# Small 32-bit products of layer 1: moving operand repeated to 96 columns

## The reference, cut to what matters

```python
# Mamba-2: 8 heads
dt = zxbcdt[..., D_INNER + CONV_DIM:]          # 8 columns of x @ in_proj_w.T
dt = softplus(dt + dt_bias); dA = exp(dt * A)  # decays: the kernel uses running sums of dt * A
y = y * rsqrt(mean(y * y, axis=-1) + 1e-05) * norm_w
# mLSTM: 4 heads
gate_in = concatenate([q, k, v], axis=-1)      # k and v are both ctx
ig = gate_in @ igate_kernel + igate_bias       # 4 columns
fg = gate_in @ fgate_kernel + fgate_bias       # 4 columns
cs = cumsum(log_sigmoid(fg), axis=tokens)
```

## Time and profile before

| | |
|---|---|
| median of 3 runs | 1158.27 us (1157.61 to 1158.8) |
| the profiled execution, own time | 1157.71 us |
| its span | 1156.0 us |
| PE busy | 1109.2 us, 96% |
| DVE busy | 824.5 us, 71% |
| ACT busy | 671.1 us, 58% |
| chain that ended last | PE 80%, DVE 11%, ACT 6% |
| mean granted TensorE clock | 0.986 of full |

### The profile page before, as it was taken

One profiled execution on the slowest core, in us unless ns is written; L12 is line 12 of the kernel. 1 busy time (PEld: TensorE's weight loads), 2 busy tenths in 40 slices (PEclk: granted clock), 3 DMA queues, 4 the chain that ended last, 5 costly groups with the idle time before them and its releaser, 6 DMA issues.

```text
span 1156.0 us, 23649 instructions
## 1 busy us (share of the span) xinstructions
PE 1109.2 (96%) x8692; PEld 922.6 (80%) x8692; DVE 824.5 (71%) x2589; ACT 671.1 (58%) x1423; POOL 324.6 (28%) x354
## 2 busy tenths in 40 slices
PE   7999999999999999999999999989999999999996
PEld 6778888768888877888867888868788887888875
DVE  5825558884668783668883767898797877887673
ACT  4237555236665436656425765586558866678573
POOL 5699956990037100026300003302000001000000
PEclk9999999999999999999999999998999989999999
DMA  8200000100000100000100201210000101000000
GB/s 335 113 19 1 2 1 1 56 20 1 2 1 2 55 20 1 2 2 2 37 20 5 73 1 46 69 51 1 2 19 2 47 1 29 19 2 28 28 20 19
DMA packets 21393, 33.33 MB, mean 29 GB/s; under 512 B 11424, under 2 KB 12192, under 8 KB 20128
## 3 DMA queue, kind: packets, MB, share of 16 engines
q1 hardware_dynamic: 21280, 31.82, 8.1%
HBM read 27.62 MB, written 4.19 MB: 28 GB/s over the span
## 4 chain that ended last, share of the span: by engine, by line
PE 80%; DVE 11%; ACT 6%; issue 2%; POOL 0%; DMA 0%; DVEq 0%; SPq 0%; ACTq 0%
PE ps L498 48%; PE ps L654 4%; PE ps L672 2%; PE ps L671 2%; PE ps L646 2%; DVE z L1631 2%; PE ps L644 2%; PE ps L670 2%; PE ps L914 2%; PE ps L513 1%; PE ps L610 1%; PE ps L701 1%; PE ps L874 1%; DVE pq L1475 1%; PE ps L623 1%
## 5 line engine op out<-in xcount | busy, mean ns | idle before, releaser
L498 PE MATMUL ps<-wts,arena 128*128 128x256 f32 (+2 forms) x1008 | 196.0, 350 | 4.8 <-ACT arena L1392 2.7
L2150 POOL TENSOR_TENSOR pq<-pq 128x512 f16<-128x512 f32 x72 | 83.9, 1166 | 406.0 <-ACT pq L1239 406.0
L498 PE MATMUL ps<-arena,wts 128*128 128x256 f16 (+1 forms) x1344 | 184.6, 290 | 8.6 <-DVE arena L1445 6.3
L498 PEld LDWEIGHTS ps<-wts,arena 128*128 128x128 f32 (+1 forms) x1008 | 149.8, 151 | 40.1 <-ACT arena L1392 3.2
L498 PEld LDWEIGHTS ps<-arena,wts 128*128 128x128 f16 (+1 forms) x1344 | 149.6, 113 | 30.4 <-DVE arena L1445 6.7
L1631 DVE SCALAR_TENSOR_TENSOR z<-ps,small,z 128x256 f32<-128x256 f32 x256 | 123.9, 484 | 22.9 <-PE ps L498 6.0
L1516 DVE CUSTOM_DVE_ANT_0 pq<-ps,mb 128x128 f32<-128x128 f32 x128 | 36.9, 288 | 106.2 <-PE ps L646 105.6
L498 PE MATMUL ps<-wts,pq 128*128 128x256 f16 x864 | 106.4, 273 | 4.5 <-DVE z L1631 1.7
L2198 POOL TENSOR_TENSOR z<-z,wts 128x512 f32<-128x512 f32 x8 | 10.3, 1282 | 318.3 <-PE ps L513 318.3
L498 PEld LDWEIGHTS ps<-wts,pq 128*128 128x128 f16 x864 | 83.4, 98 | 17.8 <-POOL pq L2150 3.4
L1236 ACT ACTIVATE pq<-ps 128x512 f32<-128x512 f32 x72 | 42.8, 595 | 83.8 <-PE ps L498 83.3
(11 more groups left out here) (290 smaller groups left out, 2488.9 us busy)
## 6 DMA issues: line engine op xcount, KB each, us to landing
cT<-in_cT SPq DMA_DIRECT2D x16, 256.0 KB, 2.7
wts<-in_up SPq DMA_DIRECT2D x1, 2304.0 KB, 18.4
wts<-in_down SPq DMA_DIRECT2D x1, 2304.0 KB, 23.8
xT<-in_xT SPq DMA_DIRECT2D x8, 256.0 KB, 4.1
xin<-in_x SPq DMA_DIRECT2D x8, 256.0 KB, 2.9
xmid<-xin SPq DMA_DIRECT2D x8, 256.0 KB, 2.0
wts<-in_w SPq DMA_DIRECT2D x2, 1024.0 KB, 4.9
wts<-in_c SPq DMA_DIRECT2D x16, 128.0 KB, 3.1
```

The costliest lines, as they stand in the source:

```text
L498: ins = mm(out_, l, r, start=(n == 0), stop=(n == len(pairs) - 1))
L2150: G.tensor_tensor(lo, abuf(s, e), hi, ALU.subtract).then_inc(*po.up(("alo", s, e)))
```

## The change

In layer 1 every product of the five steps above streams 96 columns where it streamed 8, 4 or 1. For `dt`, `gates` and the running sums the moving operand is the same 8 or 4 columns named 12 or 24 times by an access pattern with a step of 0 (`repeated`); nothing more is stored in SBUF. For the sums of squares it is 96 columns of the matrix of ones. The output of a token tile takes 96 columns of the PSUM bank, and its readers take the first 8, 4 or 1 of each 96 (`spaced`). The number of instructions, their order and their waits are as before.

```diff
--- before.py
+++ after.py
@@ -444,6 +444,14 @@
         zh = [x.bitcast(F16).rearrange("p (i k t) -> p i k t", i=2, k=KC) for x in (zh0, zh1)]
         cbm, csT, v1, hc = (cbm0, cbm1), (ct0, ct1), (v10, v11), (hc0, hc1)
         c3x = [c3x_.bitcast(BF16)[0:96, s * T:s * T + T] for s in range(NS)]
+
+        WIDE = 96
+
+        def repeated(x, n, w=WIDE):
+            return x.unsqueeze(1).to_broadcast([P, w // n, n])
+
+        def spaced(x, n, w=WIDE):
+            return x[:, 0:TT * w].rearrange("p (t x) -> p t x", t=TT)[:, :, 0:n]
 
         def zbuf(g, s):
 
@@ -856,9 +864,10 @@
             def cumsum(s, key, src, n):
 
                 o = take((key, s), (key, s, "out"))
-                mm(o[:, 0:n], le[:, 0:P], src[:, 0, :], start=True, stop=True)
-                mm(o[:, n:2 * n], onesq[:, :], src[:, 0, :], start=True, stop=False)
-                mm(o[:, n:2 * n], le[:, 0:P], src[:, 1, :], start=False, stop=True).then_inc(*pe.up((key, s)))
+                o0, o1 = (o[:, t * WIDE:(t + 1) * WIDE].rearrange("p (r e) -> p r e", e=n) for t in range(TT))
+                mm(o0, le[:, 0:P], repeated(src[:, 0, :], n), start=True, stop=True)
+                mm(o1, onesq[:, :], repeated(src[:, 0, :], n), start=True, stop=False)
+                mm(o1, le[:, 0:P], repeated(src[:, 1, :], n), start=False, stop=True).then_inc(*pe.up((key, s)))
 
             def rows_of(s, key, src, n):
 
@@ -880,8 +889,9 @@
                 eng.wait_ge(*pe.at("zTa", s, "out"))
                 o = take(("dt", s), ("dt", s, "out"))
                 for t in range(TT):
-                    ins = group(o[:, t * MH:t * MH + MH],
-                                [(xT[s][:, k, t * P:t * P + P], win[:, k, 2 * DI + 2 * DS:]) for k in range(KC)])
+                    ins = group(o[:, t * WIDE:(t + 1) * WIDE].rearrange("p (r e) -> p r e", e=MH),
+                                [(xT[s][:, k, t * P:t * P + P], repeated(win[:, k, 2 * DI + 2 * DS:], MH))
+                                 for k in range(KC)])
                 ins.then_inc(*pe.up(("dt", s)))
 
             def mamba_cb(s):
@@ -923,7 +933,8 @@
                     eng.wait_ge(*pe.at("ysq", s, m))
                 o = take(("ss", s), ("ss", s, "out"))
                 for t in range(TT):
-                    ins = group(o[:, t:t + 1], [(ysq[:, m, t * P:t * P + P], onesq[:, 0:1]) for m in range(DM)])
+                    ins = group(o[:, t * WIDE:(t + 1) * WIDE],
+                                [(ysq[:, m, t * P:t * P + P], onesq[:, 0:WIDE]) for m in range(DM)])
                 ins.then_inc(*pe.up(("ss", s)))
 
             def mlstm_gates(s):
@@ -932,9 +943,10 @@
                 o = take(("gt", s), ("gt", s, "out"))
                 for t in range(TT):
                     tk = slice(t * P, t * P + P)
-                    ins = group(o[:, t * 8:t * 8 + 8],
-                                [(cT[s][:, k, tk], gk[:, (1 + i) * KC + k, :]) for i in range(2) for k in range(KC)] +
-                                [(zT[s][:, k, tk], gk[:, k, :]) for k in range(KC)])
+                    ins = group(o[:, t * WIDE:(t + 1) * WIDE].rearrange("p (r e) -> p r e", e=8),
+                                [(cT[s][:, k, tk], repeated(gk[:, (1 + i) * KC + k, :], 8))
+                                 for i in range(2) for k in range(KC)] +
+                                [(zT[s][:, k, tk], repeated(gk[:, k, :], 8)) for k in range(KC)])
                 ins.then_inc(*pe.up(("gt", s)))
 
             def mlstm_cols(s):
@@ -1296,7 +1308,7 @@
             def mamba_rms(s):
                 r = sm(s, 7)[:, 0:TT]
                 eng.wait_ge(*act.at("ss", s))
-                A(r, psv(("ss", s))[:, 0:TT], ACT.Ln, scale=1.0 / DI, bias=eps[:, 0:1]).then_inc(
+                A(r, spaced(psv(("ss", s)), 1).rearrange("p t x -> p (t x)"), ACT.Ln, scale=1.0 / DI, bias=eps[:, 0:1]).then_inc(
                     *act.up(("ss", s, "out")))
                 eng.wait_ge(*act.own())
                 A(r, r, ACT.Exp, scale=-0.5).then_inc(*act.up(("yr", s)))
@@ -1798,7 +1810,7 @@
 
             def dt_in(s):
                 eng.wait_ge(*v.at("dt", s))
-                V_.tensor_tensor(th(sm(s, 0), MH), th(psv(("dt", s))[:, 0:2 * MH], MH), rowb(dtb, MH),
+                V_.tensor_tensor(th(sm(s, 0), MH), spaced(psv(("dt", s)), MH), rowb(dtb, MH),
                                  ALU.add).then_inc(
                     *v.up(("dt", s, "out")))
                 v.mark(("dtx", s, "x"))
@@ -1814,7 +1826,7 @@
 
             def mamba_steps(s):
                 eng.wait_ge(*v.at("cs", s))
-                V_.tensor_scalar(sm(s, 4), psv(("cs", s))[:, 0:2 * MH], -1.0, None, ALU.mult).then_inc(
+                V_.tensor_scalar(th(sm(s, 4), MH), spaced(psv(("cs", s)), MH), -1.0, None, ALU.mult).then_inc(
                     *v.up(("cs", s, "out")))
 
             def taps(s, m0):
@@ -1896,7 +1908,7 @@
 
             def mlstm_in(s):
                 eng.wait_ge(*v.at("gt", s))
-                V_.tensor_tensor(th(sx(s, 0), 8), th(psv(("gt", s))[:, 0:16], 8), rowb(gb, 8), ALU.add).then_inc(
+                V_.tensor_tensor(th(sx(s, 0), 8), spaced(psv(("gt", s)), 8), rowb(gb, 8), ALU.add).then_inc(
                     *v.up(("gt", s, "out")))
                 v.mark(("fg", s, "x"))
 
@@ -1907,9 +1919,9 @@
 
             def mlstm_a(s):
                 eng.wait_ge(*v.at("cs2", s))
-                V_.tensor_tensor(th(sx(s, 6), LH), th(sx(s, 0), 8)[:, :, 0:LH], th(psv(("cs2", s))[:, 0:8], LH),
+                V_.tensor_tensor(th(sx(s, 6), LH), th(sx(s, 0), 8)[:, :, 0:LH], spaced(psv(("cs2", s)), LH),
                                  ALU.subtract).then_inc(*v.up(("a", s)))
-                V_.tensor_copy(sx(s, 9), psv(("cs2", s))[:, 0:8]).then_inc(*v.up(("cs2", s, "out")))
+                V_.tensor_copy(th(sx(s, 9), LH), spaced(psv(("cs2", s)), LH)).then_inc(*v.up(("cs2", s, "out")))
 
             def mlstm_scan(s):
                 eng.wait_ge(*v.at("ar", s))
```

## The result

| | before | changed |
|---|---|---|
| median of 13 runs each | 1158.33 us (1153.12 to 1163.35) | 1148.63 us (1146.55 to 1154.22) |
| the profiled execution, own time | 1157.71 us | 1150.76 us |
| its mean granted clock | 0.986 | 0.998 |

The ratio is 0.9922, with a 95% interval of 0.9902 to 0.9942: 0.8% faster, 9.7 us between the medians. The forecast was 1147.7 us. In what follows two executions are left out, 3761.6 and 1275.0 us, both of the kernel with wide gates alone, whose ten others lie between 1151.9 and 1156.5.

What follows compares the result with a forecast made beforehand. PE was taken to bound the kernel, above all in layer 1. 13.5 us of clock given back, less 2.6 for DVE and 0.3 for readers, made 10.6: 1158.3 - 10.6 = 1147.7 us, range 1143 to 1155.

Steps and rivals of the forecast that it cites:

- The clock falls behind narrow passes, not behind rest: Layer 1, PE: five half-clock stretches, 27.2 us in all, follow closely spaced passes that stream next to nothing, with PE busy.
- its counterexample at 1058.5: Window 1058.5 to 1061.9: gates' passes followed at once by passes of 256 columns, and the clock holds.
- The rule about idle gaps: Rival: the clock follows something other than moving columns, such as idle gaps; falls stay, 1158 us; chance 0.08.
- A pass costs the same at 96 columns: The 480 widened PE passes: the weight load sets 0.111 us each as before, so the extra columns cost 0.
- The rival of slow repeated columns: 352 passes reading with a step of 0 take 0.16 us instead of 0.111; 1165 us; chance 0.06.
- 13.5 us given back: PE, layer 1: the five half-clock stretches pass in half the time, 13.6 us, less half of 0.27 us waited.
- DVE takes 2.6 us of it: In the five stretches PE may wait for DVE: bounds 0 and 5.2 us, the middle, 2.6, taken.
- the falls only move: Rival: PE waits more for DVE and ACT, bringing new half-clock stretches; 1153 to 1156 us; chance 0.14.
- Readers pay 0.3 us: Readers of 40 product groups wait for a later last pass: 0.3 us taken, 0.4 to 3.2 if all on path.
- The sum: Whole kernel: 13.5 - 2.6 - 0.3 = 10.6 us less, a median of 1147.7 us, 0.9% faster.

## Why the prediction was right, step by step

- *The clock falls behind narrow passes, not behind rest.* Shown three ways for the gates: six falls of six behind them where they alone are narrow, none in nine profiles where they are wide, and a clock of 0.9956 with narrow gates once other instructions stream beside them. For dt with the running sums the mean clock shows it, for the squares only the places of the falls. This was the step on which all hung, and from the trace of before it was only an inference; its counterexample at 1058.5 was the luck of one profile. The falls at 1089.0 here and 1137.0 before stand behind a gap in PE's work (PE busy for 0.04 of 3.10 and 1.48 of 3.40 us). The rule about idle gaps (the Trainium skill, TensorE: Matmul & The Clock Gate, "Why this matters for your kernels") agrees with these two in kind; for the falls behind gates, with PE busy 3.40 of 3.40 us, it doesn't, so that rival is gone.
- *A pass costs the same at 96 columns.* Forecast 0.111 us, measured 0.112. The rival of slow repeated columns is refuted by the kernel with different columns, and doubling shows where it would begin to cost.
- *13.5 us given back.* In the profiled pair it was 27.2 us of half clock down to none in the same places: right. Over many runs the clock went from 0.986 to 0.997 and not to 0.998; of the changed kernel's two profiles one has a fall behind a wait and one has none. 0.0109 x 1156 = 12.6 us.
- *DVE takes 2.6 us of it.* PE's waits for DVE grew by 2.7 us and its idle time in layer 1 by 3.6, as forecast (2 to 3, under 6), though 1.7 of the 2.7 is the one wait at 1084.7 (1.32 before, 3.06 after). The pair lost more than that in all: 1.2 us were lost in the first stretch and 1.3 behind the third, about 1.4 went in small pieces, and the spot before 1089 took 3.1, half of it by a new fall that I had as a rival ("the falls only move"); against it 1.0 came from 1137.0. The sum had no term for what began this loss, the late write of an output for which DVE waits; in the second profile, where the write is in time, the execution took 1146.6 us. Over many runs 81% of lost PE work reaches the end, which is 2.4 us of 12.6: as a mean my 2.6 was near, in this pair it was not. That is in part luck: 2.6 was the middle of two bounds, worked out from DVE's work alone, and PE's waits for DVE are 10.0 us in the second profile, 0.7 more than before.
- *Readers pay 0.3 us.* Not measured alone. By the line of time on clock, 0.9971 would be 1148.1 us for the kernel before; the changed one has 1149.5. The 1.4 us can be this cost (bound 3.2), or DVE and the late write, which take more from a PE that runs ahead. That the line flattens near full clock is not what the runs show: the changed kernel's is steeper, 1.20 against 0.94 us for 0.001. This stays open.
- *The sum.* 10.6 us forecast; 9.7 between the medians of 13 runs, 8.8 between the means of 35 and 13 runs.

What the prediction did not say is how wide the runs scatter: the three runs that it had span 1.2 us, the 13 and more measured since 10 and more. The falls themselves are scattered.

## What to carry to other kernels

When PE is the bound, look at the granted clock by windows, and at each fall ask first what PE did before it: if it was busy with short products of few columns whose pace the weight load sets, more columns are free up to that pace and can hold the clock. Look at several profiles before you name a place: which of the narrow stretches loses it changes from one execution to the next. Check the width against the load (here free at 96, 0.05 us a pass too much at 192). What is won on PE reaches the end only as far as the next engine lets it, here four fifths, and a PE that runs ahead and waits can lose the clock again behind the wait. When the engine it waits for stands idle itself, ask what that one waits for: here it was a write to memory.

## What the runs showed of the hardware

Time and mean granted clock go together run by run, with a correlation of -0.96 over 35 runs of one kernel, so the mean clock of a run tells a change of this kind sooner than its time does. The falls differ between executions (one at 1089.0 and none in the two profiles of the changed kernel), so a profile's list of them is one draw: I had taken the gates for 4 of 5 parts; widened alone they give 0.0062 of the clock's 0.0109, and left narrow alone they cost 0.0081 of it. An access pattern with a step of 0 on the moving operand streams as fast as different columns (0.112 us a pass both ways at 96). One write of 256 KB at the same step took 3.2 to 3.6 us in seven profiles and 4.6 to 5.7 in six.
